# A unit's ten transposes: one by one between output products instead of in a row

## What is computed

```
def _causal_attn(q, k, v, scale):
    s = jnp.einsum('bhqd,bhkd->bhqk', q, k) * scale
    mask = jnp.tril(jnp.ones((q.shape[2], k.shape[2]), dtype=bool))
    s = jnp.where(mask[None, None], s, jnp.finfo(s.dtype).min)
    p = jax.nn.softmax(s, axis=-1)
    return jnp.einsum('bhqk,bhkd->bhqd', p, v)
...
k = jnp.repeat(k, GROUPS, axis=1)
v = jnp.repeat(v, GROUPS, axis=1)
attn = _causal_attn(q, k, v, SCALE)
lat = _causal_attn(q, lk, lv, SCALE)
...
return attn @ w_o + lat @ w_lo
```

## Time and profile before

| | |
|---|---|
| median of 3 runs | 2533.32 us (2532.18 to 2535.01) |
| profiled execution | 2531.58 us, span 2529.6 us |
| TensorE busy | 2468.4 us, 98% of the span |
| DVE, ACT, POOL busy | 1734.9, 1131.9, 921.8 us |
| transposes at L1248 | 1280, with 11.7 us of idle time before them |
| granted TensorE clock, mean | 0.994 |

### The profile page before, as it was taken

How to read it: one execution, slowest core, us unless ns; L and a number is a source line. 1 busy time by engine, 2 the same in 40 slices (tenths; PEclk the granted TensorE clock), 3 DMA queues, 4 the chain that set the end, 5 groups by cost and what they waited for, 6 DMA issues and landing times.

```text
span 2529.6 us, 40729 instructions
## 1 busy us (share of the span) xinstructions
PE 2468.4 (98%) x12456; PEld 2088.7 (83%) x12456; DVE 1734.9 (69%) x3589; ACT 1131.9 (45%) x2576; POOL 921.8 (36%) x696
## 2 busy tenths in 40 slices
PE   7899999999999999999989999999999999999998
PEld 6688888888888888887767888888888888888877
DVE  5676767767676767665587676767767677667656
ACT  3444434344444535444365453544444354544551
POOL 4334242433434242432543424243342524334210
PEclk9999999999999999999999999999999999999999
DMA  5323231312223232322423323222232323234411
GB/s 179 89 80 92 64 104 58 98 56 75 87 75 95 62 98 60 90 64 87 136 89 131 105 70 109 69 85 77 83 104 71 109 70 106 60 90 147 154 34 67
DMA packets 124407, 226.26 MB, mean 89 GB/s; under 512 B 13088, under 2 KB 21408, under 8 KB 124192
## 3 DMA queue, kind: packets, MB, share of 16 engines
q1 hardware_dynamic: 119552, 216.91, 28.2%
q10 hardware_dynamic: 4768, 8.39, 0.9%
HBM read 206.37 MB, written 18.87 MB: 89 GB/s over the span
## 4 chain that ended last, share of the span: by engine, by line
PE 94%; DVE 3%; issue 1%; ACT 1%; DMA 0%; POOL 0%; SPq 0%; PEldq 0%; ACTq 0%; DVEq 0%
PE bank_a L1200 16%; PE bank_a L1202 16%; PE bank_a L1201 16%; PE bank_b L1200 13%; PE bank_b L1201 13%; PE bank_b L1202 13%; PE bank_b L1248 5%; PE bank_b L1517 1%; PE bank_a L1325 0%; DMA probs<-xt 0%; DVE probs L809 0%; PE bank_b L1384 0%; PE bank_b L1500 0%; POOL w_lo L414 0%; DVE acc L845 0%
## 5 line engine op out<-in xcount | busy, mean ns | idle before, releaser
L414 POOL TENSOR_TENSOR w_lo<-w_raw,w_hi 128x512 fp32r<-128x512 f32 x632 | 844.0, 1344 | 1419.2 <-ACT w_hi L478 1411.2
L478 ACT ACTIVATE w_hi<-w_raw 128x512 fp32r<-128x512 f32 x632 | 392.9, 626 | 287.9 <-DMA w_raw<-wstream 141.5
L1200 PE MATMUL bank_a<-w_hi,o_hi 128*128 128x512 f32 x1024 | 410.7, 401 | 9.0 <-DVE acc L845 4.8
L1202 PE MATMUL bank_a<-w_hi,o_lo 128*128 128x512 f32 x1024 | 403.5, 394 | 0.0
L1201 PE MATMUL bank_a<-w_lo,o_hi 128*128 128x512 f32 x1024 | 403.1, 394 | 0.0
L826 DVE TENSOR_TENSOR pT_lo<-bank_b,pT_hi 128x512 fp32r<-128x512 f32 (+1 forms) x384 | 207.0, 594 | 267.1 <-ACT pT_hi L521 267.1
L515 ACT ACTIVATE probs<-probs,row_min 128x512 f32<-128x512 f32 (+3 forms) x512 | 281.6, 552 | 240.8 <-DVE row_min L809 238.4
L525 ACT ACTIVATE o_hi<-bank_b 128x512 fp32r<-128x512 f32 x128 | 76.8, 600 | 455.4 <-PE bank_b L1202 455.4
L820 DVE TENSOR_SCALAR probs<-probs,row_inv 128x512 f32<-128x512 f32 (+3 forms) x512 | 261.4, 570 | 4.5
L1200 PEld LDWEIGHTS bank_a<-w_hi,o_hi 128*128 128x128 f32 x1024 | 193.5, 189 | 44.3 <-issue 7.8
L1200 PE MATMUL bank_a<-xT_hi,w_hi 128*128 128x512 f32 x544 | 214.2, 394 | 14.4 <-POOL w_lo L414 14.4
(11 more groups left out here) (176 smaller groups left out, 4785.4 us busy)
## 6 DMA issues: line engine op xcount, KB each, us to landing
w_raw<-wstream SPq DMA_DIRECT2D x632, 256.0 KB, 2.7
stage<-ctx SPq DMA_DIRECT2D x32, 256.0 KB, 2.7
stage_w<-wf SPq DMA_DIRECT2D x32, 256.0 KB, 2.8
q_scratch<-stage_q SPq DMA_DIRECT2D x32, 128.0 KB, 2.3
wf_hi_scratch<-piece_hi SPq DMA_DIRECT2D x16, 256.0 KB, 3.0
wf_lo_scratch<-stage_w SPq DMA_DIRECT2D x16, 256.0 KB, 3.3
wf_hi<-wf_hi_scratch SPq DMA_DIRECT2D x8, 512.0 KB, 7.9
wf_lo<-wf_lo_scratch SPq DMA_DIRECT2D x8, 512.0 KB, 11.8
```

Of the source, the lines that this page charges most:

```text
L414: nc.gpsimd.tensor_tensor(w_lo[:, s], w_raw[:, r], w_hi[:, s].bitcast(F32), ALU.subtract).then_inc(lo_done, 1)
L478: nc.scalar.activation(w_hi[:, s], w_raw[:, r], ACT.Copy).then_inc(hi_done, 1)
L1200: nc.tensor.matmul(dst, still[0], move[0], start=start, stop=False)
L1202: return nc.tensor.matmul(dst, still[1], move[0], start=False, stop=stop)
```

## The change

`transposes` becomes `turn(G, u, n)`, which issues one transpose. `TURNS` lists the ten in the same order as before, with a mark on those that raise `pT_ready`. The first of them carries the two waits. `output` takes a function `beside`, which it calls with the number j = 3t + part behind each of its first eleven matmuls. In the loop groups, for units 0 to 6, the first chunk calls turn j - 6 for j = 6 to 10, and the second chunk turn j + 5 for j = 0 to 4. First groups and unit 7 keep the ten in a row. The order of the other engines is untouched.

```
+TURNS = [(kt, bank, at, qt, kt != 1 and qt == TT - 1) for kt, bank, at, _ in PT for qt in range(kt, TT)]
+TURNS_FROM = 6
...
+            def turn(G, u, n):
+                if n == 0:
+                    if u + 1 < UNITS:
+                        pe.wait_ge(masked, 4 * (UNITS * G + u + 2))
+                    else:
+                        pe.wait_ge(pT_lo_done, 3 * (UNITS * G + u))
+                    pe.wait_ge(normed, 4 * (UNITS * G + u + 1))
                 row = {qt: at for qt, _, at, _ in TRI}
-                for kt, bank, at, _ in PT:
-                    for qt in range(kt, TT):
-                        src, dst = row[qt] + P * kt, at - N * bank + P * (qt - kt)
-                        last = nc.tensor.transpose(BANK_B[bank][:, dst:dst + P], probs[:, u % 2, src:src + P],
-                                                   ident_sb[:])
-                    if kt != 1:
-                        last.then_inc(pT_ready, 1)
+                kt, bank, at, qt, ends = TURNS[n]
+                src, dst = row[qt] + P * kt, at - N * bank + P * (qt - kt)
+                last = nc.tensor.transpose(BANK_B[bank][:, dst:dst + P], probs[:, u % 2, src:src + P], ident_sb[:])
+                if ends:
+                    last.then_inc(pT_ready, 1)
...
-                    last = product(BANK_A[t][:], o, weights(pos, 0, N), u == 0, u == 3)
+                    for part in range(3):
+                        last = nc.tensor.matmul(BANK_A[t][:], o[part // 2], w[part % 2],
+                                                start=u == 0 and part == 0, stop=u == 3 and part == 2)
+                        if beside is not None and 3 * t + part < 11:
+                            beside(3 * t + part)
...
+                def turn_in_first(j):
+                    if j >= TURNS_FROM:
+                        turn(G, u, j - TURNS_FROM)
+                def turn_in_second(j):
+                    if j + 11 - TURNS_FROM < len(TURNS):
+                        turn(G, u, j + 11 - TURNS_FROM)
                 for u in range(UNITS):
+                    if not first and u < UNITS - 1:
+                        part(2 * u + 2, turn_in_first)
+                        part(2 * u + 3, turn_in_second)
+                    else:
+                        if u < UNITS - 1:
+                            part(2 * u + 2)
+                        for n in range(len(TURNS)):
+                            turn(G, u, n)
+                        if u < UNITS - 1:
+                            part(2 * u + 3)
                     if u < UNITS - 1:
-                        part(2 * u + 2)
-                    transposes(G, u)
-                    if u < UNITS - 1:
-                        part(2 * u + 3)
                         values(G, u)
```

More of the change, by code:

```diff
@@ L1233, in scores @@
                     product(BANK_B[bank][:, col:col + w], q, k, True, True).then_inc(scores_ready, 1)
[L1235 to L1243, removed]
-                row = {qt: at for qt, _, at, _ in TRI}
-                for kt, bank, at, _ in PT:
-                    for qt in range(kt, TT):
-                        src, dst = row[qt] + P * kt, at - N * bank + P * (qt - kt)
-                        last = nc.tensor.transpose(BANK_B[bank][:, dst:dst + P], probs[:, u % 2, src:src + P],
-                                                   ident_sb[:])
-                    if kt != 1:
-                        last.then_inc(pT_ready, 1)
+            def turn(G, u, n):
[5 more added lines that the diff above has]
+                    pe.wait_ge(normed, 4 * (UNITS * G + u + 1))
+                row = {qt: at for qt, _, at, _ in TRI}
+                kt, bank, at, qt, ends = TURNS[n]
[3 more added lines that the diff above has]
+                    last.then_inc(pT_ready, 1)
             def values(G, u):
@@ L1275, in split, with output @@
                 pe.wait_ge(lo_done, chunk(b, g, c) + 1)
-            def output(b, g, c, pos, i, p, base, free):
+            def output(b, g, c, pos, i, p, base, free, beside=None):
                 half, u = i // 4, i % 4
                 split(b, g, c)
+                w = weights(pos, 0, N)
                 for t in range(TT):
@@ L1405, in queries_out, with prev @@
                     return rope_read, ROPES * G + HG + 1 + t + 1
-                def prev(i):
+                def prev(i, beside):
                     if first:
@@ L1412, in prev, with own @@
                         pe.wait_ge(o_lo_done, UNITS * G)
-                    output(b, g, C_PREV + i, C_PREV + i, i, p, 4, queries_out)
-                def own(i):
+                    output(b, g, C_PREV + i, C_PREV + i, i, p, 4, queries_out, beside)
+                def own(i, beside):
                     if i < 4:
@@ L1421, in own, with part @@
                         free = lambda t: (cross_summed, TT + t + 1)
-                    output(b, g, C_OWN + i, C_OWN + i, i, p + 2, 0, free)
-                def part(slot):
+                    output(b, g, C_OWN + i, C_OWN + i, i, p + 2, 0, free, beside)
+                def part(slot, beside=None):
                     if first and b and slot == 0:
@@ L1431, in part @@
                     for i in ((NEXT_PARTS if b else FIRST_PARTS)[slot] if first else (slot,)):
-                        prev(i) if i < 8 else own(i - 8)
+                        prev(i, beside) if i < 8 else own(i - 8, beside)
                 part(0)
```

## The result

The changed kernel takes 2601.78 us (median of 4 runs, 2598.86 to 2603.28) against 2534.1 of before in the same measurement: a ratio of 1.0269, 95% interval 1.0256 to 1.0281. It is **68 us slower**. The forecast was slower, 2591 with a range up to 2600, so the direction and the place were right, and the time is 11 us above the forecast and 2 us outside the range.

The account below looks back on a forecast made before the run. TensorE, holding 94% of the span, was taken to bound the kernel. Waits of 4.20 us per group, 59 over 14 groups, plus 1 direct made 60 on the profiled 2531.58: forecast 2591 us, range 2558 to 2600.

Parts of the forecast that it names:

- The wait of turn 0 in even units: First transpose, units 2, 4 and 6: masked scores ready at 1.31 us, before its start at 1.60, so no wait.
- in unit 0: First transpose of unit 0: the mask ends at 1.74 us, so TensorE waits 0.24 us per group.
- The lateness of bank b1: Bank b1 waits for turn 7 at 4.21 us, so DVE's last `pT_lo` comes 0.52 us later.
- of L820: DVE's `normalise`, making next to no progress while POOL's operation runs, ends 0.84 us later in all, at 8.55.
- The waits: TensorE idle before transposes, per group: 0.24 us in unit 0, 1.27 in 1, 1.25 in 3 and 5, 0.19 at 7.
- The direct cost: TensorE's extra time for 980 single transposes, ten weight loads uncovered as before: about +1 us, 0 to +4 possible.
- Rival 1: DVE's chain to the masks is not delayed, only the wait stands earlier: 2560 us, chance 0.08.
- Rival 2: On TensorE, interleaving hides the product's weight load behind a transpose: 2512 to 2544 us, chance 0.08.
- Rival 3: The order on TensorE's queue has no effect, neither wait nor gain: 2534 us, chance 0.03.
- The clock: TensorE keeps its granted clock of 1.00 (2.4 GHz) through pauses of this size, so nothing was added.
- What would show it: Trace signs: TensorE idle before transposes, about 59 us more; last `pT_lo` at 5.75, L820's end near 8.5, loads 0.11 apart.

Follow-up runs that it names:

- w_hi_late: The changed kernel, but in the loop groups ACT makes every second `w_hi` behind `o_hi` instead of ahead of it; 2555.14 us against 2600.05 for the changed kernel.
- a_late_start: The changed kernel with turns 0 to 4 back in a row behind the whole first chunk, 5 to 9 left single; 2554.13 us against 2533.13 before.
- b_early_banks: The changed kernel with turns 0 to 4 left single from product 6, 5 to 9 in a row between the chunks; 2559.68 us against 2533.13 before.
- row_early: The kernel before with all ten transposes still in a row, but behind product 6 of the first chunk; 2545.29 us against 2533.13 before.
- changed_again: The changed kernel itself, unaltered, measured again beside later runs on the same chip; 2600.05 us, ratio 1.0263 to the kernel before.
- small_add: The changed kernel with `add_part` cut to 32 of its 512 columns; 2547.59 us against 2532.30 for the kernel before with the same cut.

## Why the prediction was right and wrong

**The wait of turn 0 in even units** (none) and **in unit 0** (0.24): right. Unit 0 is 0.29 longer, with the direct cost in it.

**The lateness of bank b1, 0.52, and of L820, 0.84**: right. The rows give 0.59 and 0.91 (6.23 against 5.64, 8.62 against 7.71); 0.07 of each is the direct cost of the eight turns ahead. w_hi_late shows the POOL part by itself, a_late_start and b_early_banks that most of the 68 us takes both the late chain and the early wait, row_early that an early wait costs only 12 us when the banks come early with it.

**The waits**: 1.27, 1.25, 1.25 and 0.19 forecast, with 0.24 in unit 0: right. Less a direct cost of 0.08, which is what units 2 and 4 show, the means give 1.25, 1.25, 1.27, 0.21 and 0.24. Their sum is 4.2 per group (4.0 in changed_again, where units 2 and 4 show 0.10), and 4.20 was forecast.

**The direct cost was the step that failed**: 980 transposes at 0.001 apiece, +1 us, with 0 to +4 possible. It is 0.08 per unit in the changed kernel and in small_add and 0.10 in changed_again, thus 8 to 10 us in the 98 units. I took for granted that slots are the longer of streaming and next load and add up whatever stands beside them. I bounded the error by the resolution of the rows, not by a row in which a short and a long matmul alternate; the rows of `values` have short ones behind short ones. With +8 instead of +1 the sum would have been 2599. Two smaller things make up the rest of the 11 us. The later `o_lo` behind the last group of each batch entry, 1.2 us, stood nowhere in the sum. And the sum was added to the profiled execution of 2531.58, where the median before was 2534.1, 2.5 more. The range ended at 2600, which left no room for these. The second measurement of the same kernel gave 2600.05, so whether the range held was decided by less than 2 us, while the difference to before was 68 both times.

**Rival 1** (chain not delayed, 2560): excluded by the masks at 2.70; b_early_banks comes near to that case and took 2559.7. **Rival 2** (loads hidden): excluded. The load of the product behind a transpose starts with the transpose at 2250.75, 0.21 after the transpose's own load, and not with the product ahead of it. None of 12454 loads in this trace, and none of 12454 in the one before, starts earlier than the matmul just ahead of its own. The Trainium skill, "TensorE: Matmul & The Clock Gate", Step-by-step, says that loads are pulled ahead of running matmuls. In these two traces that reaches one matmul ahead and never two. **Rival 3** (no effect): excluded. The clock: 0.994 mean in both.

**What would show it**: the places and lengths of the waits were right, "about 59 us more" of idle time was wrong, since gaps in the matmul rows undercount a wait by what is left of the last product's row.

## What to carry to other kernels

A piece of work that stands in a row can be spread only as far as the engines behind it have slack: list what its first part waits for, who needs its last part, and what each of these waits for next, all against the same zero. Here the first part came earlier than its inputs, which alone cost 27 us, and the last later than its users needed, which alone cost 21; both together cost 68. And a transpose whose next weight load is not covered in a row leaves it uncovered one by one as well. Here spreading changed nothing in the number of uncovered loads and made each pair a little dearer.

## What the runs showed of the hardware

- A transpose costs 0.109 in a row, and 0.117 to 0.119 alone between two 512-column products (0.109 and a tenth of the 0.08 to 0.10 per unit); an ordinary 128-column matmul in its place costs 0.112.
- No weight load started before the matmul just ahead of its own had started, in 12454 loads before and 12454 after.
- Four in-place multiplications on DVE took 1.28 without POOL and 2.27 with the last 1.19 of a 1.29 long POOL subtraction beside their start; they ended 1.08 after it.
- TensorE stays at its granted clock of 1.00 (237.8 to 1204.0 in the changed kernel) through pauses of about 1.25 us every 22 us: the mean over the span is 0.994 with and without them.
